# Keys alone masked, head slots as stationary operands, x transposed on 64x64 tiles, deviation spread from a step-zero operand

## What is computed

```python
xn = _ln2d(x, norm1_g, norm1_b)              # mean and variance over the 64 channels
xn = jnp.roll(xn, shift=(-4, -4), axis=(2, 3))
qkv = windows @ in_w.T + in_b                # windows: 64 x (64 tokens, 64 channels)
scores = jnp.einsum('nhid,nhjd->nhij', q, k) / jnp.sqrt(8)
attn = jax.nn.softmax(scores, axis=-1)
out = jnp.einsum('nhij,nhjd->nhid', attn, v)
y = x + roll_back((out @ out_w.T + out_b) @ proj_w.T + proj_b)
z = gelu(fc1(_ln2d(y, norm2_g, norm2_b)))
return y + fc2(z)
```

## Time and profile before

| | us |
|---|---|
| median of 3 runs | 88.28 |
| lowest, highest | 87.34, 88.77 |
| span of the profiled execution | 86.4 |
| TensorE busy | 79.8 |
| VectorE busy | 66.7 |
| GpSimd busy | 53.3 |
| ScalarE busy | 51.1 |

### The profile page before, as it was taken

One profiled execution on the slowest core, in us unless ns is written; L12 is line 12 of the kernel. 1 busy time (PEld: TensorE's weight loads), 2 busy tenths in 40 slices (PEclk: granted clock), 3 DMA queues, 4 the chain that ended last, 5 costly groups with the idle time before them and its releaser, 6 DMA issues.

```text
span 86.4 us, 3871 instructions
## 1 busy us (share of the span) xinstructions
PE 79.8 (92%) x1578; PEld 46.1 (53%) x1578; DVE 66.7 (77%) x216; ACT 51.1 (59%) x85; POOL 53.3 (62%) x64
## 2 busy tenths in 40 slices
PE   5999999987999999899999989999999999999950
PEld 5988657444666665664666635554554423223420
DVE  4998998989989979989989987999762964333160
ACT  0296798976358836858578366354588556634400
POOL 7988828995593980899696596896908044800000
PEclk9999999999999999999999999999999999999998
DMA  0999510111010111111111202000000000031142
GB/s 19 206 337 441 231 38 0 34 61 52 31 52 31 46 53 49 53 46 38 46 52 39 66 17 67 31 8 0 8 0 0 0 8 0 0 121 68 53 156 91
DMA packets 3617, 5.72 MB, mean 66 GB/s; under 512 B 1072, under 2 KB 1840, under 8 KB 3472
## 3 DMA queue, kind: packets, MB, share of 16 engines
q1 hardware_dynamic: 2736, 3.08, 11.0%
q10 hardware_dynamic: 864, 2.40, 7.4%
HBM read 2.66 MB, written 1.05 MB: 43 GB/s over the span
## 4 chain that ended last, share of the span: by engine, by line
PE 66%; DVE 21%; issue 8%; ACT 1%; DVEq 0%; ACTq 0%
PE ps_s L323 12%; PE ps_u L414 8%; PE ps_t L275 6%; PE ps_u L484 5%; DVE row_max L644 4%; DVE stats L624 3%; PE ps_t L323 3%; PE ps_t L468 3%; PE ps_t L397 3%; PE ps_m L323 3%; PE ps_s L468 2%; PE ps_m L297 2%; PE ps_o L428 2%; PE ps_o L484 2%; DVE sums L663 2%
## 5 line engine op out<-in xcount | busy, mean ns | idle before, releaser
L1047 POOL TENSOR_TENSOR max_x<-max_t,early 128x512 bf16<-128x512 bf16 x14 | 14.7, 1047 | 9.7 <-DVE max_t L657 9.7
L644 DVE TENSOR_REDUCE row_max<-ps_s 128x16 f32<-128x1024 f32 x15 | 18.1, 1209 | 1.5 <-PE ps_s L323 1.2
L919 ACT ACTIVATE probs<-ps_t 128x1024 f32<-128x1024 f32 x13 | 13.3, 1024 | 8.9 <-PE ps_t L397 8.4
L323 PE MATMUL ps_s<-masked,qk 32*64 32x256 f32 x240 | 16.6, 387 | 1.6 <-DVE row_max L644 0.6
L323 PE MATMUL ps_t<-masked,qk 32*64 32x256 f32 x224 | 15.3, 387 | 0.0
L1056 POOL TENSOR_TENSOR rstd<-y_var,minus_half 128x4 f32<-128x4 f32 x8 | 8.3, 1034 | 6.9 <-DVE y_var L707 6.9
L323 PEld LDWEIGHTS ps_s<-masked,qk 32*64 32x64 f32 x240 | 7.9, 131 | 6.1 <-issue 2.4
L414 PE MATMUL ps_u<-probs,vz 128*32 128x64 f32 x512 | 10.6, 222 | 0.0
L414 PEld LDWEIGHTS ps_u<-probs,vz 128*32 128x32 f32 x512 | 8.0, 109 | 3.4 <-issue 3.0
L1032 POOL TENSOR_TENSOR rstd<-var,minus_half 128x4 f32<-128x4 f32 x8 | 8.6, 1076 | 1.0 <-DVE var L632 0.4
L275 PE MATMUL ps_t<-zeros 128*128 128x128 f32 x32 | 7.1, 389 | 1.0 <-DVE zeros L818 1.0
(11 more groups left out here) (114 smaller groups left out, 149.9 us busy)
## 6 DMA issues: line engine op xcount, KB each, us to landing
masked<-qk SPq DMA_DIRECT2D x54, 32.0 KB, 1.9
x_ch<-x_ch_d ACTq DMA_DIRECT2D x1, 1024.0 KB, 8.1
out_d<-result SPq DMA_DIRECT2D x3, 256.0 KB, 2.5
x_tok<-x_tok_d ACTq DMA_DIRECT2D x1, 512.0 KB, 6.1
late<-late_d ACTq DMA_DIRECT2D x1, 352.0 KB, 5.3
x_tok<-x_tok_d SPq DMA_DIRECT2D x2, 128.0 KB, 3.4
x_tok<-x_tok_d ACTq DMA_DIRECT2D x1, 256.0 KB, 4.9
out_d<-result SPq DMA_DIRECT2D x2, 128.0 KB, 2.3
```

Source lines behind the costliest of these rows:

```text
L323: return nc.tensor.matmul(ps[o:o + L, g, n * TOK:(n + 1) * TOK], qk[r:r + RG, b, w, t], masked[r:r + RG, b, :, w, t], start=(n == 0), stop ...
L644: nc.vector.tensor_reduce(row_max[:, w, 0:16], score_bank(k, w)[:].rearrange("q g (h j) -> q (g h) j", j=L), axis=AX.X, op=ALU.max).then_i ...
L919: nc.scalar.activation(probs[:, w, :], scores_t_bank(k, w)[:].rearrange("q g c -> q (g c)"), ACT.Exp).then_inc(probs_done, 1)
L1047: nc.gpsimd.tensor_tensor(max_x[:, k % 2, w, :].rearrange("q (n i) -> q n i", n=16), bf16_high(max_t[:, w, :]).unsqueeze(1).to_broadcast([ ...
```

## The change

`masked` holds keys alone, in half as many buffers. Queries stay unmasked. Tiles alternate between the two halves of the rows: `q_rows(k)` puts queries at rows 0 to 63 and keys at 64 to 127 for even k, and the other way round for odd k, and masked keys go to the rows of the queries. `scores` keeps its form. `scores_t` now has masked keys of one head slot as stationary operand and 64 moving columns of `qk`, one matmul for each of four slots (`score_t_unit`, called by `scores_t_block`), 32 in place of 8. `mask_q_first` goes. The bias of the projection has a column for either order. `x_transpose` is eight matmuls on 64x64 tiles against the identity, written to both banks of `ps_m`, in place of two transposes. `y_spread` is eight matmuls (four for the last two tiles) whose stationary operand is the deviation itself with a step of zero over 32 (64) columns; `ln2_widen` goes, the spread lands in `ps_o` for most tiles, and all spreads and `ln2_scale` stand at one place in each slot. The lines below leave out declarations, waits of the setup and the host's packing.

```diff
@@ -219,6 +215,15 @@
         def tokens(k):
             return slice(k * TOK, (k + 1) * TOK)
 
+        def q_rows(k):
+            return C * (k % 2)
+
+        def k_rows(k):
+            return C - q_rows(k)
+
+        def masked_keys(k, h, w):
+            return masked[q_rows(k):q_rows(k) + C, k // 2 % 2, h, w]
+
         def score_bank(k, w):
             return ps_t if k == 0 and w == 1 else ps_s
 
@@ -231,9 +236,9 @@
             return [(0, STEP // 2), (STEP // 2, STEP)] if s == STEPS - 1 else [(0, STEP)]
 
         def spread_bank(k):
-            if k < TILES - 4:
-                return ps_m[:, 1, :]
-            return (ps_u[:, 0, 0:], ps_u[:, 0, TOK:], ps_o[:, 0, 0:], ps_o[:, 0, TOK:])[k - TILES + 4]
+            if k < TILES - 3:
+                return ps_o[:, 0, TOK:2 * TOK]
+            return (ps_u[:, 0, TOK:2 * TOK], ps_o[:, 0, 0:TOK], ps_o[:, 0, TOK:2 * TOK])[k - TILES + 3]
 
         def fc1_bank(s, m):
             return (ps_s, ps_t, ps_m)[(2 * s + m) % 3]
...
@@ -245,22 +250,20 @@
 
         @block.sync
         def _(sp):
-            def mask_heads(k, dst, src, done, heads=SLOTS):
-                b = k % QB
+            def mask_keys(k, heads=SLOTS):
                 sp.wait_ge(qk_copied, k + 1)
                 if k < QB:
-                    sp.wait_ge(masked_zeroed[k], 1)
+                    sp.wait_ge(masked_zeroed[k // 2], 1)
                 else:
                     sp.wait_ge(scores_shifted, 2 * (k - QB) + 2)
                 for h in range(heads):
-                    sp.dma_start(masked[dst + h:dst + C:SLOTS, b, h], qk[src + h:src + C:SLOTS, b]).then_inc(done, 16)
+                    sp.dma_start(masked[q_rows(k) + h:q_rows(k) + C:SLOTS, k // 2 % 2, h],
+                                 qk[k_rows(k) + h:k_rows(k) + C:SLOTS, k % QB]).then_inc(k_masked[k % QB], 16)
 
             for i, (a, b) in enumerate(XTOK[:2]):
                 sp.dma_start(x_tok[:, a * TOK:b * TOK], x_tok_d[:, a * TOK:b * TOK]).then_inc(xtok_loaded[i], 16)
-            mask_heads(0, C, 0, q_masked[0], 2)
             for k in range(1, TILES):
-                mask_heads(k, 0, C, k_masked[k % QB], 2 if k in (1, 2) else SLOTS)
-                mask_heads(k, C, 0, q_masked[k % QB])
+                mask_keys(k, 2 if k == 1 else SLOTS)
             for s in range(STEPS):
                 for i, (a, b) in enumerate(store_parts(s)):
                     sp.wait_ge(result_done, s + 1 + i)
...
@@ -283,18 +286,22 @@
                 if k >= 1:
                     pe.wait_ge(v_copied, 2 * k)
                 for n in range(BLK):
-                    ins = nc.tensor.transpose(ps_m[:, 0, n * P:(n + 1) * P],
-                                              xhat[:, k % 2, n * P:(n + 1) * P], ident)
+                    for u in range(2):
+                        r = slice(L * u, L * u + L)
+                        for w in range(2):
+                            c = n * P + C * w
+                            ins = nc.tensor.matmul(ps_m[C * w:C * w + C, u, n * L:(n + 1) * L],
+                                                   xhat[r, k % 2, c:c + C], ident[r, L * u:L * u + L],
+                                                   start=True, stop=True, tile_position=(L * u, C * w))
                 ins.then_inc(x_transposed, 1)
 
             def project_qk(k):
                 pe.wait_ge(xn_copied, k + 1)
-                if k >= 2 * AHEAD + 1:
-                    pe.wait_ge(z_done, k - 2 * AHEAD)
                 for w in range(2):
                     r = slice(C * w, C * w + C)
                     for s in range(2):
-                        ins = nc.tensor.matmul(ps_m[C * s:C * s + C, w, 0:TOK], w_qkv[r, C * s:C * s + C],
+                        c = (q_rows(k), k_rows(k))[s]
+                        ins = nc.tensor.matmul(ps_m[C * s:C * s + C, w, 0:TOK], w_qkv[r, c:c + C],
                                                xn[r, k % 2, :], start=True, stop=True, tile_position=(C * w, C * s))
                 ins.then_inc(qk_projected, 1)
 
...
@@ -315,37 +322,40 @@
                 project_qk(k)
                 project_v(k)
 
-            def score_unit(ps, base, stationary, k, w, n, g, u):
-                b = k % QB
-                r = base + RG * g
+            def score_unit(k, w, n, g, u):
+                r = q_rows(k) + RG * g
                 t = slice((2 * n + u) * L, (2 * n + u + 1) * L)
-                o = L * (u if base else u ^ g)
-                return nc.tensor.matmul(ps[o:o + L, g, n * TOK:(n + 1) * TOK], qk[r:r + RG, b, w, t],
-                                        masked[r:r + RG, b, :, w, t], start=(n == 0), stop=True,
+                o = L * (u ^ g)
+                return nc.tensor.matmul(score_bank(k, w)[o:o + L, g, n * TOK:(n + 1) * TOK], qk[r:r + RG, k % QB, w, t],
+                                        masked[r:r + RG, k // 2 % 2, :, w, t], start=(n == 0), stop=True,
                                         skip_group_check=True, tile_position=(r, o))
+
+            def score_t_unit(j, w, n, h, g, u):
+                r = q_rows(j) + RG * g
+                t = slice((2 * n + u) * L, (2 * n + u + 1) * L)
+                c = n * TOK + h * L
+                return nc.tensor.matmul(scores_t_bank(j, w)[L * u:L * u + L, g, c:c + L],
+                                        masked[r:r + RG, j // 2 % 2, h, w, t], qk[r:r + RG, j % QB, w, t],
+                                        start=(n == 0 and h == 0), stop=True,
+                                        skip_group_check=True, tile_position=(r, L * u))
 
             def scores_ready(k, w):
                 if k == 0:
...
-                    pe.wait_ge(k_masked[k % QB], 64 * (k // QB) + (0, 32, 32, 64)[k % QB])
-                if k in (1, 2) and w == 0:
-                    pe.wait_ge(k_masked_dve, 2 + k)
+                    pe.wait_ge(k_masked[k % QB], 64 * (k // QB) + (0, 32, 64, 64)[k % QB])
+                if k == 1 and w == 0:
...
@@ -365,19 +381,15 @@
                 for n in range(BLK):
                     for g in range(2):
                         for u in range(2):
-                            ins = score_unit(ps_s, 0, qk, k, w, n, g, u)
+                            ins = score_unit(k, w, n, g, u)
                     if n == BLK - 1:
                         ins.then_inc(scores_done, 1)
-                    for g in range(2):
-                        for u in range(2):
-                            score_unit(scores_t_bank(j, v), C, qk, j, v, n, g, u)
+                    scores_t_block(j, v, n)
 
             def scores_t(j, w):
                 scores_t_ready(j, w)
                 for n in range(BLK):
-                    for g in range(2):
-                        for u in range(2):
...
@@ -439,19 +453,20 @@
                 ins.then_inc(y_summed, 1)
 
             def y_spread(k):
-                pe.wait_ge(y_rstd_wide, k + 1)
-                if k < 2:
-                    pe.wait_ge(v_copied, 2 * (k + 2 * AHEAD + 1))
-                    if k == 1:
-                        pe.wait_ge(z_done, 1)
-                elif k < TILES - 4:
-                    pe.wait_ge(probs_done, 2 * (k + 4))
-                elif k == TILES - 4:
+                pe.wait_ge(y_rstd_done, k + 1)
+                if k < TILES - 3:
+                    pe.wait_ge(y_done, k + 2)
+                elif k == TILES - 3:
                     pe.wait_ge(sums_transposed, TILES)
-                elif k == TILES - 2:
+                else:
                     pe.wait_ge(y_var_done, TILES)
-                for n in range(BLK):
-                    ins = nc.tensor.transpose(spread_bank(k)[:, n * P:(n + 1) * P], rstd2_x[:, k % 2, n, :], ident)
+                cols = 32 if k < TILES - 2 else C
+                for b in range(BLK):
+                    for c in range(0, P, cols):
+                        out = spread_bank(k)[c:c + cols].rearrange("q (j b i) -> q j b i", j=4, b=BLK)
+                        ins = nc.tensor.matmul(out[:, :, b, :],
+                                               rstd2[:, k % 2, b, c // C:c // C + 1].to_broadcast([P, cols]), ident,
+                                               start=True, stop=True, tile_position=(0, c))
                 ins.then_inc(y_rstd_spread, 1)
 
             def fc1(s, m):
...
@@ -535,8 +550,6 @@
                     scores_t(t, 0)
                 if t == 1:
                     x_transpose(AHEAD + 1)
-                if t >= TILES - 2:
-                    y_spread(t - AHEAD - 1)
                 shift_scores(t, 0)
                 if t == 1:
                     weigh_values(0, 1)
@@ -555,9 +568,9 @@
                     bias_of_v()
                 if tile_ok(t + AHEAD + 1):
                     x_transpose(t + AHEAD + 1)
-                if AHEAD <= t < TILES - 3:
+                weigh_values(t, 0)
+                if t >= AHEAD:
                     y_spread(t - AHEAD)
-                weigh_values(t, 0)
                 if t >= 2:
                     y_sum(t - 2)
 
@@ -565,6 +578,10 @@
```

(49 more changed lines are left out.)

54 lines of the change are left out of this document (24 added, 30 removed).

## The result

The changed kernel takes 108.19 us (median of 4 runs, 106.5 to 109.17) where the kernel before takes 88.44 us in the same comparison: ratio 1.217, 95% interval 1.201 to 1.233. The profiled execution of the changed kernel has a span of 106.8 us; that of before had 86.4.

What follows compares the result with a forecast made beforehand. Bound taken: TensorE's instruction supply, one block of 256 per 3.95 us. 15.2 + 17 x 3.95 = 82.4, plus 23.1 behind slot 7 = 105.5 span, plus 1.9 to the median = 107 us; range 98 to 116.

Steps and rivals of the forecast that it cites:

- T: Least time TensorE needs per block of 256 instructions, set by fetching them: 3.95 us, mean of 4.37 and 3.58.
- The 17 steps: From block 2 in scores_t(0, 0) to block 19 at the end of weigh_values(7, 0): 17 x 3.95 us.
- the first term: Start of TensorE's instruction block 2, in scores_t(0, 0), held until its fetch is there: 15.2 us.
- the second: The 17 block steps up to the end of weigh_values(7, 0), each at 3.95 us.
- The array time: In scores_both, 64 narrow products take 0.92 us beside the wide ones, against 1.05 now: nearly even.
- The array serializes: Rival: in scores_both narrow products wait behind wide ones or take turns; +0.3 us each likely, 92 us; chance 0.05.
- Each product has a turn of its own: Rival: each TensorE product has its own turn, dearer than 18 ns, at 27.5 ns; 100 us; chance 0.02.
- The sign set down for the array: Sign of a wrong forecast: a scores_both taking 1.3 us or more without a gap.
- the signs of the supply: 20 packets, 256 records per 3.6 to 4.4 us, TensorE below 80%, issue gaps, restarts 1.25 us after fetches, VectorE/ScalarE idle.
- The transposes: x_transpose on 64x64 tiles: 0.23 us against 0.37, saving 0.14 to 0.24 us, five times on the path.
- Supply keeps up: Rival: TensorE's instruction blocks are fetched further ahead, so the account of work holds: 87.5 us; chance 0.07.
- The clock: Rival: TensorE standing still 1.6 us of every 4 lowers its clock to half, 11 us on top, 118; chance 0.02.

Runs made afterwards that it cites:

- e2: The changed kernel with its transposed scores back in one product of 256 columns for four of 64, leaving out three of four head slots; 89.07 us.
- e3: The kernel before with only x transposed on 64x64 tiles and the step-zero deviation spread, no widening; scores and masks as before; 88.72 us, ratio 1.012.
- e1: The kernel before with only each transposed-score matmul split into 4 of 64 columns, masked queries still moving; 101.48 us, ratio 1.156.
- e12: The changed kernel with probs and vz held in bf16, 512 TensorE instructions less; 100.96 us, ratio 1.133.

## Why the prediction was right

**The bound.** "An edit that adds TensorE instructions without adding TensorE work is not free here" was the step that carried it, and it held: 20 packets, 3.87 us for a block where 3.95 was taken, restarts 1.25 to 1.56 us behind the end of a fetch where 1.25 was read from two cases. That T came out within 2% is partly luck: it was the mean of 4.37 and 3.58, and single steps of the changed kernel run from 3.5 to 4.4. Six kernels with different instructions in the blocks gave 3.69 to 3.99.

**The sum.** Block 2 was entered at 17.04, not 15.2: its fetch was early enough (it was there 2.9 us ahead), and TensorE's work ahead of it set the time. Blocks 2 to 5 came at the pace of the work as well, 29.31 - 17.04 = 12.27 us for three, of which waits for the first masks are a part. The 17 steps took 66.45 us against 67.15. Behind them lay 23.3 us against 23.1. Span 106.8 against 105.5; the first term was 1.8 too low, the second 0.7 too high, which partly cancel.

**The array time, the step that failed.** "In array time this is nearly even" was wrong. I took 14 ns per product from 16 that followed a run of others, and set 64 narrow products (0.92) beside the wide ones as if in parallel. The 64 alone take 1.08 us, 17 ns each, and a `scores_both` takes 1.67 for 1.05 us: the two kinds run neither wholly side by side (1.08) nor one after the other (1.08 and the 1.09 of 16 wide ones alone, 2.2). Two of the rivals speak to this. *The array serializes* had +0.3 us as its likely size and +1.0 as its end, and +0.62 lies between. *Each product has a turn of its own* is borne out in that 32 columns cost what 64 do, at 17 to 21 ns and not 27.5; but it is no fixed turn, since 32 products of 256 columns take 1.05 us (33 ns each), 48 take 1.27 (26) and 80 take 1.67 (21). Which of the two it is stays open. The sign set down for the array, a `scores_both` of 1.3 us or more without a gap, did show, beside all but one of the signs of the supply. Alone it would have given 88.4 - 0.8 + 8.7 = 96 us. It did not show in the time because a block of such work still needs less than 3.87 us: the 12.5 us of pauses are what is left (108.2 - 12.5 = 95.7). The forecast of the time was right with this term 9 us off, since only the larger of two bounds counts.

**The busy share.** I wrote that TensorE's would fall below 80%. It is 87%, down from 92. Of 106.8 us 14.0 are not busy. The pauses are longer than their idle time: that before 53.03 is 1.66 us from start to start and counts 1.28 as idle, since the ends of products are modelled. And the work between the pauses had grown too. The Trainium skill, "Perfetto Trace Analysis", section Identifying the Most-Contended Engine, says that the matmul busy share is no good measure of how close TensorE is to its limit. The trace agrees: the share fell by 5 points where 12.5 us of pauses came in.

**The transposes and the rest.** `x_transpose` takes 0.33 us from its start to the next group's (49.51 to 49.84), not 0.23, so it saved 0.04 and not 0.14. GpSimd's and SP's work was gone from the path at no gain, as costed: neither e2 nor e3, which have less of it, is faster than before in the median.

**The rivals.** Supply keeps up: out by e1, by the steps of about 253 records in e12, and by the restarts behind each fetch. The clock: 1.00 in every window read of the changed kernel, through idle stretches of up to 1.3 us.

## What to carry over

Count the instructions of each stretch, not only its work, and look for the instruction queue in the DMA part: packets of 256 TensorE instructions, and a stop of the engine in the middle of a run with no load in flight, were the signs of this bound here. It was one block per 3.7 to 4.0 us, 15 ns per instruction, so a split of wide products into narrow ones has two prices: 0.62 us of array time for 48 products more, and their 96 instructions, 1.45 us at 15 ns. The two do not add: the 8.7 us of array work that the forecast had left out did not lengthen the changed kernel, because the supply was the slower of the two. That work taken out of such a kernel gains nothing unless its instructions go too would follow, but no run here shows it.

## What was not expected of the hardware

- The supply of instructions in the changed kernel, on average: 1.34 us until the next block's fetch starts, 1.13 us of transfer, 1.40 us until its first product.
- Narrow products of 32x64 tiles take the same time with 32 and with 64 columns: 1.64 and 1.67 us for a `scores_both`. Their order does not matter either: 1.68 us when wide and narrow ones alternate.
- Met waits, six in a row, cost TensorE 0.108 us each, most of it at the lower clock; 17 single ones taken out gave nothing.
- One wait of 1.76 us was followed by 8.4 us of work at a lowered clock (mean 0.59), one of 0.64 us was not, and the idle stretches of up to 1.3 us in the changed kernel left it at 1.00.
